# Attention in a three-part transformer kernel: softmax sums turned by a trip through DRAM, and V's high and low parts side by side in one stationary tile

## The reference, cut to what matters

```python
def attention(x, ctx, Wq, Wk, Wv, Wo, bo):
    b, n, _ = x.shape
    m = ctx.shape[1]
    q = (x @ Wq).reshape(b, n, HEADS, D_HEAD)          # 16 heads of 64
    k = (ctx @ Wk).reshape(b, m, HEADS, D_HEAD)
    v = (ctx @ Wv).reshape(b, m, HEADS, D_HEAD)
    sim = jnp.einsum('bihd,bjhd->bhij', q, k) * SCALE
    attn = jax.nn.softmax(sim, axis=-1)
    out = jnp.einsum('bhij,bjhd->bihd', attn, v).reshape(b, n, HEADS * D_HEAD)
    return out @ Wo + bo
...
h = layernorm(x, ln1_g, ln1_b)
x = attention(h, h, a1_Wq, a1_Wk, a1_Wv, a1_Wo, a1_bo) + x
h = layernorm(x, ln2_g, ln2_b)
x = attention(h, context, a2_Wq, a2_Wk, a2_Wv, a2_Wo, a2_bo) + x
```

## Time and profile before

| | us |
|---|---|
| median of three runs | 1088.32 (1087.79 to 1089.55) |
| the profiled execution, whole | 1088.15 |
| its span, first to last instruction | 1086.4 |
| TensorE busy | 997.5 (92%) |
| VectorE busy | 710.9 (65%) |
| ScalarE busy | 626.5 (58%) |
| GpSimd busy | 357.2 (33%) |

### The profile page before, as it was taken

One profiled execution on the slowest core, in us unless ns is written; L12 is line 12 of the kernel. 1 busy time (PEld: TensorE's weight loads), 2 busy tenths in 40 slices (PEclk: granted clock), 3 DMA queues, 4 the chain that ended last, 5 costly groups with the idle time before them and its releaser, 6 DMA issues.

```text
span 1086.4 us, 21327 instructions
## 1 busy us (share of the span) xinstructions
PE 997.5 (92%) x7872; PEld 937.3 (86%) x7872; DVE 710.9 (65%) x1598; ACT 626.5 (58%) x1945; POOL 357.2 (33%) x474
## 2 busy tenths in 40 slices
PE   5688874599999999999999999999999998899998
PEld 4577753489999999899999899999999997899998
DVE  4466744596766676667667775666677667566664
ACT  3466452386656575657566765666666666533333
POOL 1101324033334333333333244454554454401010
PEclk9999887699999999999999998999999999999999
DMA  6221000100200000000000300300000001010100
GB/s 205 68 68 39 20 20 20 44 11 2 98 2 21 1 21 1 21 1 21 2 21 3 101 25 1 103 25 2 25 26 18 8 21 46 17 38 21 40 30 21
DMA packets 28121, 34.62 MB, mean 32 GB/s; under 512 B 2164, under 2 KB 21364, under 8 KB 28020
## 3 DMA queue, kind: packets, MB, share of 16 engines
q1 hardware_dynamic: 28020, 33.26, 9.9%
HBM read 24.86 MB, written 8.39 MB: 31 GB/s over the span
## 4 chain that ended last, share of the span: by engine, by line
PE 79%; DVE 10%; ACT 6%; issue 2%; POOL 1%; DMA 1%; SPq 1%; DVEq 0%; POOLq 0%
PE bank L1306 17%; PE bank L1307 16%; PE bank L1308 16%; PE bank L1523 8%; PE bank L1506 5%; PE bank L1564 3%; PE bank L1565 3%; PE bank L1566 3%; PE bank L1538 3%; ACT p L721 1%; PE bank L1480 1%; PE bank L1414 1%; DVE bn L887 1%; PE bank L1415 1%; PE bank L1416 1%
## 5 line engine op out<-in xcount | busy, mean ns | idle before, releaser
L721 ACT ACTIVATE p<-bank,negmax 128x256 f32<-128x256 f32 (+1 forms) x512 | 208.2, 428 | 18.0 <-DVE negmax L1088 15.1
L538 POOL TENSOR_TENSOR oT_hi<-oT,ones 128x256 fp32r<-128x256 f32 x128 | 94.0, 735 | 378.0 <-DVE oT L1111 378.0
L731 ACT CAST pT_hi<-bank 128x512 fp32r<-128x512 f32 (+1 forms) x256 | 110.7, 485 | 166.1 <-PE bank L1523 165.3
L1306 PE MATMUL bank<-hT_hi,w_hi 128*128 128x256 f32 x640 | 190.6, 298 | 5.9 <-DVE hT_lo L1072 2.5
L1308 PE MATMUL bank<-hT_hi,w_lo 128*128 128x256 f32 x640 | 181.5, 284 | 0.0
L1307 PE MATMUL bank<-hT_lo,w_hi 128*128 128x256 f32 x640 | 181.3, 283 | 0.0
L1306 PEld LDWEIGHTS bank<-hT_hi,w_hi 128*128 128x128 f32 x640 | 122.6, 192 | 9.2 <-DVE hT_lo L1072 4.8
L1103 DVE TENSOR_TENSOR pT_lo<-bank,pT_hi 128x512 fp32r<-128x512 f32 (+1 forms) x256 | 129.7, 548 | 0.3
L1084 DVE TENSOR_REDUCE negmax<-bank 128x2 f32<-128x512 f32 x128 | 82.2, 684 | 66.8 <-PE bank L1506 66.8
L1307 PEld LDWEIGHTS bank<-hT_lo,w_hi 128*128 128x128 f32 x640 | 122.9, 192 | 0.0
L1308 PEld LDWEIGHTS bank<-hT_hi,w_lo 128*128 128x128 f32 x640 | 122.6, 192 | 0.0
(11 more groups left out here) (200 smaller groups left out, 2787.2 us busy)
## 6 DMA issues: line engine op xcount, KB each, us to landing
w_stage<-in_weights SPq DMA_DIRECT2D x52, 256.0 KB, 4.8
x_in<-x_dram SPq DMA_DIRECT2D x24, 256.0 KB, 2.9
x_dram<-x_out SPq DMA_DIRECT2D x16, 256.0 KB, 3.2
l_x<-in_x SPq DMA_DIRECT2D x4, 512.0 KB, 5.6
x_dram<-l_out SPq DMA_DIRECT2D x4, 512.0 KB, 2.9
out_dram<-x_out SPq DMA_DIRECT2D x8, 256.0 KB, 3.1
l_ctx<-in_ctx SPq DMA_DIRECT2D x4, 240.0 KB, 5.3
ctx_in<-in_ctx SPq DMA_DIRECT2D x8, 120.0 KB, 3.2
```

The costliest lines, as they stand in the source:

```text
L538: nc.gpsimd.tensor_tensor(oh[:, G % PAIRS, :], of[:, :], ones[:, :], ALU.mult).then_inc(y["o_hi"], 1)
L721: last = nc.scalar.activation(p[:, G % 2, e, t * cols:(t + 1) * cols], scores_at(G, e, t), ACT.Exp, bias=negmax[:, G % 2, t, e:e + 1], acc ...
L731: nc.scalar.copy(pTh[0:r, G % 2, e, 0:n], bank[4 + e][0:r, 0:n]).then_inc(y["pT_hi"], 1)
L1306: nc.tensor.matmul(dst, lh, rh, start=(i == 0), stop=False)
```

## The change

The reciprocal sums no longer go through POOL, PE and ACT. SP writes them to a small DRAM tensor, waits until they have landed, and reads them back with two DMAs that give each of 64 partitions the same 256 numbers (`spread_sums`). This runs once a step, and SP's loads, stores and weight units are put at given steps between them. V's high and low parts of a head lie next to each other in one tile `v_hi_lo`, 128 columns for a head. A matmul with that tile gives the product with the high part in 64 rows and with the low part in the other 64, for each head in its own half of bank 6. ACT copies the low halves out (`copy_low_values`, two copies of 64 rows), DVE adds them to the high halves (`add_low_values`, two additions of 64 rows), and POOL does the multiplication by the reciprocal sums ahead of the split (`split_o`). `oT` and `rsumT` have two buffers now. The zeros in the V tiles and their 16 memsets (L1279) are gone.

```diff
--- before.py
+++ after.py
@@ -30,7 +30,7 @@
-VW = 3 * DH
+VW = 2 * DH
@@ -212,17 +212,17 @@
-                vh = sb("v_hi", [128, NT, PAIRS * VW], F32R, where=att)
-                vl = sb("v_lo", [128, NT, PAIRS * VW], F32R, where=att)
+                vv = sb("v_hi_lo", [128, NT, HEADS * VW], F32R, where=att)
-                rsw = sb("rsum_wide", [128, 2, NT, 2 * DH], where=att)
-                rT = sb("rsumT", [128, S], where=att)
-                of = sb("oT", [128, S], where=att)
+                rT = sb("rsumT", [128, 2, S], where=att)
+                ob = sb("oT_low_values", [128, S], where=att)
+                of = sb("oT", [128, 2, S], where=att)
+                on = sb("oT_scaled", [128, S], where=att)
@@ -310,10 +311,11 @@
-        def v_dst(buf, b, c):
-
-            half = slice(c % 2 * 4 * VW, (c % 2 + 1) * 4 * VW)
-            return buf[0:v_rows(b), c // 2, half].rearrange("p (g s d) -> p g s d", g=4, s=3)[:, :, 0:3:2, :]
+        def v_dst(b, c, low):
+
+            part = vv[0:v_rows(b), c // 2, c % 2 * 4 * 2 * VW:(c % 2 + 1) * 4 * 2 * VW]
+            part = part.rearrange("p (g s d) -> p g s d", g=4, s=4)
+            return part[:, :, 1:3, :] if low else part[:, :, 0:4:3, :]
@@ -429,24 +431,45 @@
+            def spread_sums(G):
+
+                sp.wait_ge(y["rsum"], G + 1)
+                if G >= 2:
+                    sp.wait_ge(y["rT"], 32 * (G - 1))
+                sp.dma_start(sums_dram[G % 2, :, :].rearrange("e (q t) -> q e t", t=NT),
+                             rs[:, G % 2, :].rearrange("q (e t) -> q e t", e=2)).then_inc(y["rsum_row"], 16)
+                sp.wait_ge(y["rsum_row"], 16 * (G + 1))
+                if G >= 2:
+                    sp.wait_ge(y["o_norm"], G - 1)
+                for e in range(2):
+                    sp.dma_start(rT[e * DH:(e + 1) * DH, G % 2, :], sums_dram[G % 2, e:e + 1, :].partition_broadcast(DH)
+                                 ).then_inc(y["rT"], 16)
+
...
-            for b in range(3 * B):
-                if b + 3 < 3 * B:
-                    load(b + 3)
+            for G in range(STEPS):
+                b, i = divmod(G, PAIRS)
+                spread_sums(G)
+                if i == 3 and b >= 1:
+                    store(b - 1)
+                if i == 4:
+                    load(b + 2)
+                if i == 5 and B < b + 2 < 2 * B:
+                    load_context(b + 2)
+                if b == 1 and i < 4:
+                    load_weights(sp, 12 + i, 13 + i)
+                if b == B - 1 and i >= 2 and i < 6:
+                    load_weights(sp, 14 + i, 15 + i)
+                if b == B + 1 and i < 4:
+                    load_weights(sp, 20 + i, 21 + i)
+                if b == 2 * B - 1 and i in (6, 7):
+                    load_weights(sp, 18 + i, 19 + i)
+            store(2 * B - 1)
+            for b in range(2 * B, 3 * B):
+                if b + 2 < 3 * B:
+                    load(b + 2)
                 store(b)
-                if B < b + 3 < 2 * B:
-                    load_context(b + 3)
-                if b == 0:
-                    load_weights(sp, 12, 16)
-                if b == 6:
-                    load_weights(sp, 16, 20)
-                if b == 8:
-                    load_weights(sp, 20, 24)
-                if b == 14:
-                    load_weights(sp, 24, 26)
@@ -526,23 +549,23 @@
                                         row(phase_of(b).bias).unsqueeze(1).broadcast_to([128, NT, D]),
                                         ALU.add).then_inc(y["xb"], 1)
-            def widen_sums(G):
-                pool.wait_ge(y["rsum"], G + 1)
-                nc.gpsimd.tensor_tensor(rsw[:, G % 2, :, :].rearrange("p t (e d) -> p (t e) d", e=2),
-                                        rs[:, G % 2, :].unsqueeze(2).broadcast_to([128, NT * 2, DH]),
-                                        ones[:, :].rearrange("p (n d) -> p n d", d=DH), ALU.mult
-                                        ).then_inc(y["rsum_wide"], 1)
-
             def split_o(G):
+                pool.wait_ge(y["o_sum"], G + 1)
+                pool.wait_ge(y["rT"], 32 * (G + 1))
+                if G >= 1:
+                    pool.wait_ge(y["o_lo"], G)
+                nc.gpsimd.tensor_tensor(on[:, :].rearrange("p (t q) -> p t q", t=NT),
+                                        of[:, G % 2, :].rearrange("p (t q) -> p t q", t=NT),
+                                        rT[:, G % 2, :].rearrange("p (q t) -> p t q", t=NT),
+                                        ALU.mult).then_inc(y["o_norm"], 1)
                 pool.wait_ge(y["o_norm"], G + 1)
-                nc.gpsimd.tensor_tensor(oh[:, G % PAIRS, :], of[:, :], ones[:, :], ALU.mult).then_inc(y["o_hi"], 1)
+                nc.gpsimd.tensor_tensor(oh[:, G % PAIRS, :], on[:, :], ones[:, :], ALU.mult).then_inc(y["o_hi"], 1)
                 pool.wait_ge(y["o_hi"], G + 1)
-                nc.gpsimd.tensor_tensor(ol[:, G % PAIRS, :], of[:, :], oh[:, G % PAIRS, :].bitcast(F32),
+                nc.gpsimd.tensor_tensor(ol[:, G % PAIRS, :], on[:, :], oh[:, G % PAIRS, :].bitcast(F32),
                                         ALU.subtract).then_inc(y["o_lo"], 1)
             def step(G):
                 b, i = divmod(G, PAIRS)
-                widen_sums(G)
                 if i == 0:
                     inverse_std(b + 1)
                 if i == 3:
@@ -730,9 +753,13 @@
-            def copy_rT(G):
+            def copy_low_values(G):
+
-                nc.scalar.copy(rT[:, :], bank[6][:, S:2 * S]).then_inc(y["rT_copied"], 1)
+                if G >= 1:
+                    act.wait_ge(y["o_sum"], G)
+                nc.scalar.copy(ob[0:DH, :], bank[6][DH:128, 0:S])
+                nc.scalar.copy(ob[DH:128, :], bank[6][0:DH, S:2 * S]).then_inc(y["o_low"], 1)
@@ -1093,7 +1120,9 @@
             def inverse_sums(G):
                 dve.wait_ge(y["exp"], 2 * G + 2)
-                nc.vector.reciprocal(rs[:, G % 2, :], expsum[:, G % 2, :, :].rearrange("p t e -> p (t e)")
+                if G >= 2:
+                    dve.wait_ge(y["rsum_row"], 16 * (G - 1))
+                nc.vector.reciprocal(rs[:, G % 2, :].rearrange("p (e t) -> p e t", e=2), expsum[:, G % 2, :, :].rearrange("p t e -> p e t")
                                      ).then_inc(y["rsum"], 1)
             def pT_low(G):
@@ -1104,11 +1133,13 @@
-            def normalise_o(G):
-                dve.wait_ge(y["rT_copied"], G + 1)
-                if G >= 1:
-                    dve.wait_ge(y["o_lo"], G)
-                nc.vector.tensor_tensor(of[:, :], bank[6][:, 0:S], rT[:, :], ALU.mult).then_inc(y["o_norm"], 1)
+            def add_low_values(G):
+                dve.wait_ge(y["o_low"], G + 1)
+                if G >= 2:
+                    dve.wait_ge(y["o_norm"], G - 1)
+                nc.vector.tensor_tensor(of[0:DH, G % 2, :], bank[6][0:DH, 0:S], ob[0:DH, :], ALU.add)
+                nc.vector.tensor_tensor(of[DH:128, G % 2, :], bank[6][DH:128, S:2 * S], ob[DH:128, :], ALU.add
+                                        ).then_inc(y["o_sum"], 1)
@@ -1143,7 +1174,7 @@

             def values_low(b, c):
                 dve.wait_ge(y["v_hi"], value_product(b, c))
-                nc.vector.tensor_tensor(v_dst(vl, b, c), v_src(b, c), v_dst(vh, b, c).bitcast(F32),
+                nc.vector.tensor_tensor(v_dst(b, c, True), v_src(b, c), v_dst(b, c, False).bitcast(F32),
                                         ALU.subtract).then_inc(y["v_lo"], 1)

             def step_self(G):
@@ -1274,10 +1305,6 @@
-            for v_ in (vh, vl):
-                for pr in range(PAIRS):
-                    last = nc.vector.memset(v_[:, :, pr * VW + DH:pr * VW + 2 * DH].bitcast(F32), 0.0)
-            last.then_inc(zeros_ready, 1)
@@ -1526,25 +1553,22 @@
                     last.then_inc(y["pT"], 1)
             def weighted_values(G):
+
                 b, g = divmod(G, PAIRS)
                 cols = cols_of(G)
-                r = min(cols, 128)
-                pe.wait_ge(y["rsum_wide"], G + 1)
-                if G == 0:
-                    pe.wait_ge(zeros_ready, 1)
+                r, tiles = min(cols, 128), NT if cols == S else 1
                 if G >= 1:
-                    pe.wait_ge(y["o_norm"], G)
-                for t in range(NT):
-                    nc.tensor.transpose(bank[6][:, S + t * 128:S + (t + 1) * 128], rsw[:, G % 2, t, :], ident[:, :])
-                terms = []
-                for e in range(2):
-                    for j in range(NT if cols == S else 1):
-                        vc = slice(g * VW + e * DH, g * VW + e * DH + 128)
-                        pc = slice(j * S, (j + 1) * S)
-                        terms.append(((vh[0:r, j, vc], vl[0:r, j, vc]), (pTh[0:r, G % 2, e, pc], pTl[0:r, G % 2, e, pc])))
+                    pe.wait_ge(y["o_sum"], G)
                 pe.wait_ge(y["pT_lo"], 2 * G + 2)
                 pe.wait_ge(y["v_lo"], values_until(b, g))
```

(6 more changed lines are left out.)

## The result

The changed kernel takes 1143.44 us (median of 4 runs, 1132.57 to 1145.6) against 1088.05 us of the kernel before in the same runs: a ratio of 1.0498, 95% interval 1.0436 to 1.056. Forecast were 1057 us and a gain.

A forecast was written before the change was run, and what follows sets the result against it. PE was taken to set the pace in both attentions, with DVE nearly level in cross attention. From 1088.15 us, - 43.3 - 5.4 + 1.0 + 2.0 + 14.4 = - 31.3 gave 1057 us, range 1040 to 1074.

The forecast's parts named there:

- The sums' trip: SP's write and two reads through DRAM each step: 5.9 to 10.3 us, counted at nothing against GpSimd's 9.2 us.
- Rival D: SP's trip becomes the bound, a step lasting the write's landing plus three issues: about 1165 us, chance 0.09.
- Self attention, -43.3: Products with V in self attention: six matmuls fewer a step save 0.71 us in 61 steps, 43.3 us.
- Cross attention at full clock, -0.9 a batch: Regular cross batches: steps 5 to 7 gain 1.4 us, 0.5 is lost earlier; net 5.4 us over six.
- The forecast wait: PE's wait before step 4's product with V in a cross batch grows from 0.88 to 2.3 us.
- The clock, three falls at 4.8 us = 14.4: Regular cross batches: the grown wait drops PE to half clock in three of six, 14.4 us lost.
- Rival B: The clock falls in five or six regular cross batches: 1066.5 to 1071 us, chance 0.16.
- The first cross batch, counted at nothing: The first batch of cross attention, which already has a 2.02 us wait: no gain or loss counted.
- The last, +1.0: Last cross batch: steps 4 to 6, bound by DVE, each get an addition more, 1.0 us lost.
- Weight unit 24, +2.0: Near the end: this unit, issued behind step 6's sums, lands 2 to 4 us late, counted as 2 us.
- The 5.6 us held ready for GpSimd's stride: POOL's stride-two read of the sums, at twice the price, delays cross step 1's output projection: 5.6 us in all.
- the prediction's 4.9 us: Estimate of the sums' trip using the skill's fixed DMA cost of about 2.0 us, instead of 5.9 us.

The follow-up runs named there:

- e3_piped: The changed kernel with all its arithmetic, but SyncE writes step G's sums and then reads back those of step G-1; 1092.83 us.
- e1_no_trip: The changed kernel without the trip through DRAM, the spread reciprocals filled with ones once; 1093.14 us.
- e4_filler: e3_piped plus 20 unused matmuls ahead of step 4's product with V in each cross batch but the last; 1072.32 us.
- e6_one_add: e3_piped with one ScalarE copy and one VectorE addition over 128 partitions a step, in place of two each over 64; 1065.32 us.
- e9_moved_filler: e5_moved plus 10 unused matmuls in step 4 of each cross batch but the last (22 in the first); 1059.83 us.
- e8_coarse_write: The changed kernel, trip still serial, reciprocals written as one run of 16 bytes a partition instead of two of 8; 1095.34 us.
- e11_half_write: The changed kernel, trip still serial, only one head's reciprocals written, 128 pieces of 8 bytes instead of 256; 1162.67 us.
- e5_moved: e3_piped with ScalarE's and VectorE's work reordered in cross steps 3 and 4, so step 4's awaited addition comes earlier; 1071.22 us.
- e10_before_later: The kernel before with four unused maxima added on VectorE in cross attention's step 3; 1132.06 us.
- e7_before_late: The kernel before with two unused maxima added on VectorE in cross attention's step 3; 1097.58 us.

## Why the prediction was wrong, step by step

- **The sums' trip, "counted at nothing": the step that failed.** The landing was put at 2.5 us, the row of a DMA "with nothing in front of it". It was 4.2 us in the median: about 3.0 for the 8-byte pieces with nothing ahead, the rest from standing behind SP's own reads and other transfers. And it was compared with the wrong thing, the 9.2 us until GpSimd needs the sums of one step. What counts is how often SP can go round. Cost: 52.8 us (1143.8 - 1091.0, the spans of the change and of e3_piped), 34.2 in cross attention, 10.1 in self attention, 6.8 at the end, the rest ahead of the first batch.
- **Rival D** had that mechanism, the rule "landing plus three issues" (4.2 + 1.4 = 5.6; measured 5.4) and the point where it turns (3.9 us), at a chance of 0.09. Its term at 4.2 us, 64 x (5.6 - 4.6) = 64 us, stands for cross attention alone, where the trip cost 34.2: without the trip these steps took 5.3 us (42.30 / 8), not 4.6. So it is near the 52.8 of the whole kernel in part by luck. What it lacked was a bound for w from both sides: the 4.7 us row was set aside because it stood in a queue, and so did each write of the change.
- **Self attention, -43.3: measured -30.3.** The regular steps came as worked out: 5.45 became 4.75, 6.40 became 5.70. Only step 3 gained 0.41 in place of 0.71. Of the 13 us 7.0 are missing in the first batch (49.1 us in e1_no_trip, 47.8 before), 3.6 in the last (52.4, 52.3) and 2.3 in the six between. In the first and the last VectorE converts weight units and each step got 0.56 us more; in the first the clock also fell once for 3.4 us (e4_filler, the same work there without that fall, took 47.6). With one addition in place of the pair 8.9 us come back (e6_one_add).
- **Cross attention at full clock, -0.9 a batch: +1.1** (38.86 us in the median batch of e4_filler, 37.75 before). Steps 5 to 7 gained 1.16 (forecast 1.4). Steps 0 to 4 lost 2.26 (forecast 0.5), which fits 4 x 0.56: the pair of additions mis-sized, and VectorE, which sets the pace there, passing on all of it. With one addition and at full clock a batch took 36.67 us (e6_one_add, one batch), so the pair and its second copy cost 2.2 us of the 38.86, what the fillers may add included. The forecast wait was met (2.26 us) because further waits stand ahead of it (for the layer norm, the split and the queries, 1.5 us), not because the sum was right.
- **The clock, three falls at 4.8 us = 14.4: measured six at 3.4 us = 20.6** (42.30 - 38.86 a batch). The mechanism was right, the frequency wrong: of four waits of 2 us in the kernel before, two had been followed by a fall, and I took the same share for six batches. Three of the four stood in one batch, so they were hardly a sample; a wait like it in every batch took the clock down in every batch. Rival B, at 0.16, had five or six falls.
- **The first cross batch, counted at nothing: +1.3** (46.95 us in e3_piped, 45.68 before). **The last, +1.0: +3.4** (37.42, 34.01), with a fall of 20.5 us that begins in it instead of one of 3.4. **Weight unit 24, +2.0: the end is +3.2** with the trip overlapped, where ScalarE waited 2.4 us for that unit, and +10.0 in the change, where it waited 10.9 us; how much of either the unit accounts for isn't isolated. The 5.6 us held ready for GpSimd's stride weren't needed: its multiplication took 0.742 us.
- **Together**, against the span before: -43.3 - 5.4 + 14.4 + 1.0 + 2.0 = -31.3 was forecast. Without the trip it is -30.3 (self) + 32.0 (cross) + 3.2 (end), about +5, and e3_piped's span is 4.6 us longer. The trip adds 52.8. With the clock held and the order mended (e9_moved_filler) it is 28.4 us less: -28.1, -4.8 and +4.6.

That SyncE's waiting sets the pace of the trip is shown by e3_piped, and that 8-byte pieces do it by e8_coarse_write and e11_half_write. That the wait ahead of step 4's product takes the clock down is shown by e4_filler and e5_moved together and, in reverse, by e10_before_later. How much wait it takes isn't settled: 1.70 us with no other wait in the batch led to a fall in one batch of six (e7_before_late), 1.20 us with 1.5 us of others to two (e5_moved), and 1.28 and 1.38 us with 0.5 to 0.6 us of others to one each (e6_one_add).

## What to carry to other kernels

A queue's engine that waits for its own transfer to land has a period: landing plus issues. Compare it with the shortest step that the change leaves, not with the time until the data are needed; and where it is near, issue the next write before waiting for the last, or make its pieces longer. When an engine makes TensorE wait, price what follows at half clock too: here it was worth 3.4 us a batch, more than the wait, and filling the wait with unused matmuls or moving 1.3 us of VectorE's work by one step bought 20 us. An addition on half the partitions cost as much as on all here (0.41 to 0.43 us for 64 and for 128); splitting one in two doubled it.

## What the runs showed of the hardware

- A DRAM write of 128 partitions x 8 bytes (e11_half_write) or 2 x 8 bytes (the change) landed in 4.4 and 4.2 us, one of 128 x 16 bytes (e8_coarse_write) in 1.6 (medians of the DMA tables); its issue took 0.54 and 0.33 us. The 2 x 8 bytes landed in 3.1 us in e3_piped, where SP had issued nothing for over 1 us ahead of 126 of the 128 writes. The Trainium skill, DMA: Bandwidth & Descriptors (Specifications), sets the border for read-modify-write at 512 B. Both kinds lie below it and differ here by a factor of 2.6, or 2.1 with nothing just ahead (3.04 and 1.42 us), so that rule alone didn't tell them apart. The Trainium skill's fixed cost of about 2.0 us, on which the prediction's 4.9 us rested, is given there (Anatomy of one DMA) for DMAs that GpSimd issues. These were issued by SyncE, and the 1.6 us measured are below it.
- TensorE's granted clock fell to 0.50 (1.2 GHz) for 6.8 or 10.2 us in each of six batches, with step-4 waits of 1.7 to 2.5 us and smaller ones (e3_piped), and with 2.88 us alone (e10_before_later). In e10_before_later it fell 0.4 to 0.9 us before the wait ended, and the engine then worked without a stop.
- VectorE's `hT_lo` (128 x 512) took 1.08 us in the cross batches of before and 1.27 to 1.49 us in seven of eight of e3_piped, beside GpSimd's `x_plus_bias`, and 0.68 us in e7_before_late with GpSimd idle. In the changed kernel it took 0.69 to 1.28 us, once 0.70 beside `x_plus_bias` too. No experiment isolates it.
